# AdaLN plus mixture-of-LoRA feed-forward in split fp32: two of three column groups as a seven-product 2x2 block product per pair of tiles

## The reference

```
h   = gelu(gelu(cond @ W0 + b0) @ W1 + b1);  att = softmax(h @ W2 + b2)       # 32 x 8
y_b = (sum_k att[b,k] weight[k]) @ x_b + sum_k att[b,k] bias_k[k]             # 64x64 mix of channels per batch
p   = softmax(y @ gate_W.T); keep the top 2 of 8 experts, renormalised to w
out = x + y @ W_base.T + sum_e 2 w_e (y @ A_e.T) @ B_e                         # 1024 -> 1024, LoRA rank 8
```

## Time and profile before

| | |
|---|---|
| median of 3 runs | 257.17 us (257.11 to 258.16) |
| profiled execution, its own time | 257.24 us |
| its span, first to last instruction | 255.5 us |
| PE, PEld busy | 250.4 (98%), 243.0 (95%) us |
| DVE busy | 127.6 us (50%) |
| ACT busy | 87.7 us (34%) |
| POOL busy | 9.5 us (4%) |
| HBM | 137 GB/s over the span |
| mean granted TensorE clock | 1.000 |

### The profile page before, as it was taken

How to read it: one execution, slowest core, us unless ns; L and a number is a source line. 1 busy time by engine, 2 the same in 40 slices (tenths; PEclk the granted TensorE clock), 3 DMA queues, 4 the chain that set the end, 5 groups by cost and what they waited for, 6 DMA issues and landing times.

```text
span 255.5 us, 4274 instructions
## 1 busy us (share of the span) xinstructions
PE 250.4 (98%) x1456; PEld 243.0 (95%) x1456; DVE 127.6 (50%) x400; ACT 87.7 (34%) x205; POOL 9.5 (4%) x27
## 2 busy tenths in 40 slices
PE   8999999999999999999999999999999999999993
PEld 5899989898999999999999999999999999999992
DVE  2998643374845554345355444445545434535342
ACT  4677675816141231413132141324123141313120
POOL 6000042000000000000000000000000000000000
PEclk9999999999999999999999999999999999999999
DMA  6999868040551606051240706033060705122022
GB/s 176 406 403 316 346 176 305 17 164 3 225 185 48 201 1 246 1 176 70 86 160 0 246 0 227 19 117 129 38 208 0 244 3 174 75 87 77 3 82 82
DMA packets 10921, 35.27 MB, mean 138 GB/s; under 512 B 1264, under 2 KB 1824, under 8 KB 10912
## 3 DMA queue, kind: packets, MB, share of 16 engines
q1 hardware_dynamic: 10912, 35.15, 39.5%
HBM read 26.73 MB, written 8.39 MB: 137 GB/s over the span
## 4 chain that ended last, share of the span: by engine, by line
PE 98%; DVE 1%; issue 0%; POOL 0%; DVEq 0%; POOLq 0%
PE z_ps L764 25%; PE z_ps L765 25%; PE z_ps L766 25%; PE o_ps L783 3%; PE o_ps L789 3%; PE o_ps L788 3%; PE o_ps L780 3%; PE o_ps L778 3%; PE t_ps L843 2%; PE s_ps L813 1%; PE o_ps L764 1%; PE o_ps L765 1%; PE o_ps L766 1%; PE t_ps L804 0%; PE o_ps L892 0%; DVE z_lo L539 0%
## 5 line engine op out<-in xcount | busy, mean ns | idle before, releaser
L764 PE MATMUL z_ps<-w_hi,xt_hi 128*128 128x366 f32 (+1 forms) x376 | 125.8, 335 | 0.0
L765 PE MATMUL z_ps<-w_lo,xt_hi 128*128 128x366 f32 (+1 forms) x376 | 124.2, 330 | 0.0
L766 PE MATMUL z_ps<-w_hi,xt_lo 128*128 128x366 f32 (+1 forms) x376 | 124.0, 330 | 0.0
L764 PEld LDWEIGHTS z_ps<-w_hi,xt_hi 128*128 128x128 f32 x376 | 70.8, 188 | 0.7 <-issue 0.6
L765 PEld LDWEIGHTS z_ps<-w_lo,xt_hi 128*128 128x128 f32 x376 | 71.0, 189 | 0.2 <-issue 0.2
L766 PEld LDWEIGHTS z_ps<-w_hi,xt_lo 128*128 128x128 f32 x376 | 70.7, 188 | 0.0
L539 DVE TENSOR_TENSOR z_lo<-z_ps,z_hi 128x366 fp32r<-128x366 f32 (+1 forms) x47 | 25.3, 538 | 82.1 <-ACT z_hi L397 82.0
L397 ACT ACTIVATE z_hi<-z_ps 128x366 fp32r<-128x366 f32 (+1 forms) x47 | 22.4, 476 | 123.6 <-PE z_ps L766 123.6
L554 DVE TENSOR_TENSOR xt_lo<-xt_raw,xt_hi 128x1024 fp32r<-128x1024 f32 x14 | 17.2, 1225 | 17.7 <-ACT xt_hi L387 17.7
L617 DVE TENSOR_TENSOR out_sb<-o_ps,x_nat 128x366 f32<-128x366 f32 (+1 forms) x44 | 19.9, 505 | 4.5 <-PE o_ps L789 3.8
L778 PE MATMUL o_ps<-z_hi,blk_hi 128*128 128x366 f32 (+1 forms) x48 | 16.2, 338 | 0.0
(11 more groups left out here) (111 smaller groups left out, 178.8 us busy)
## 6 DMA issues: line engine op xcount, KB each, us to landing
x_nat<-x_in SPq DMA_DIRECT2D x16, 512.0 KB, 4.7
out<-out_sb SPq DMA_DIRECT2D x15, 512.0 KB, 3.0
xt_raw<-xt_in SPq DMA_DIRECT2D x14, 512.0 KB, 5.2
w_nat<-wn_in SPq DMA_DIRECT2D x8, 512.0 KB, 4.7
w_raw<-wext_in SPq DMA_DIRECT2D x8, 366.0 KB, 8.9
w_raw<-wext_in SPq DMA_DIRECT2D x4, 364.0 KB, 5.8
xt_raw<-xt_in SPq DMA_DIRECT2D x4, 256.0 KB, 5.4
par<-small_in SPq DMA_DIRECT2D x1, 576.0 KB, 7.2
```

The costliest lines, as they stand in the source:

```text
L764: nc.tensor.matmul(dst, hi, w_cols(w_hi, g, k), start=(k == 0), stop=False)
L765: nc.tensor.matmul(dst, hi, w_cols(w_lo, g, k), start=False, stop=False)
L766: last = nc.tensor.matmul(dst, lo, w_cols(w_hi, g, k), start=False, stop=(k == KC - 1))
```

## The change

Pairs 0 and 1 (tiles 0 to 3) stay as they were but for the following: lora_b always has 128 rows (bias rows zero until they are loaded, one small DMA for each of three rows and tile), and DVE and ACT make four sums of weight blocks there: `t_sum` (8 DVE subtractions of 128x732), `t_high` (8 ACT copies), `t_low` (8 DVE subtractions; the last four of them in the first part of pair 2).

From pair J0 = 2 on, both tiles of a pair are one unit. Let X be [[x0a, x0b], [x1a, x1b]] (tiles 0 and 1 of the pair, halves a and b of the contraction) and W the same for column groups 1 and 2. X @ W is made with seven block products of 12 matmuls (Winograd's form) in place of eight: four sums of x blocks (s_1 to s_4, 128x512; `ss_add` on DVE, `ss_high` on ACT, `ss_low` on DVE), four sums of weight blocks, and five `u_step` additions on DVE of 128x366 that join partial sums in PSUM with running sums u2, u3, c22 in SBUF. Group 0 (gate and A) stays a plain product (`z_zero`). `gating2` does the gating of both tiles with one set of instructions. Buffers of the new data lie over w_raw, w_nat and par, which are used up by then. SP reloads x tiles after the last sum that reads them.

Below, q = j - J0. `NP, NU, NO, NS = 7, 5, 6, 4` are the increments a pair of p_done, u_done, zz_hi/zz_lo/oo_done/ll_done/emptied, and s_*. Parts for the first and last pair are cut.

```diff
+            def ss_add(q, n):
+                a, b, op = {1: (xt_raw[:, 1, 0:D // 2], xt_raw[:, 1, D // 2:D], ALU.add), ...}[n]
+                nc.vector.tensor_tensor(s_raw[...][:, :], a, b, op).then_inc(s_added, 1)
+            def ss_low(q, n):                       # waits for ss_high n; s_lo = s_raw - s_hi
+            def xx_low(n, parity):                  # waits for xx_high; as x_low_next, 128x1024
+            def bb_low(q, t, parity):               # waits for bb_high; as block_low
+            def zz_low(n, src, g):
+                dve.wait_ge(zz_hi, n)
+                nc.vector.tensor_tensor(z_cols(z_lo, g), src, z_cols(z_hi, g).bitcast(F32), ALU.subtract).then_inc(zz_lo, 1)
+            def empty(n, bank, parity, g):          # waits for ll_done n; as one group of add_out
+            def u_step(out, a, b):
+                nc.vector.tensor_tensor(out[:, :], a[:, :], b[:, 0:WB], ALU.add).then_inc(u_done, 1)
+            def pair(j, ...):                       # DVE
+                    dve.wait_ge(p_done, NP * q)
+                    u_step(u2, u2, bank_c)
+                    xx_low(2 * q + 1, 1)
+                    zz_low(NO * q - 1, u2[:, :], 2)
...
+                    ss_add(q, 1)
+                    empty(NO * q - 3, o_ps[2], 0, 2)
+                    zz_low(NO * q, c22[:, :], 2)
+                    ss_add(q, 2)
+                    ss_low(q, 1)
+                    zz_low(NO * q + 1, bank_z[:, 0:WIDTH[0]], 0)
+                    empty(NO * q - 2, bank_f0, 1, 0)
+                    empty(NO * q - 1, o_ps[1], 1, 1)
+                    empty(NO * q, o_ps[2], 1, 2)
+                ss_low(q, 2)
+                ss_add(q, 3)
+                bb_low(q, 2 * j, 0)
+                bb_low(q, 2 * j + 1, 1)
+                ss_low(q, 3)
+                ss_add(q, 4)
+                zz_low(NO * q + 2, bank_c[:, 0:WIDTH[0]], 0)
+                ss_low(q, 4)
+                dve.wait_ge(p_done, NP * q + 2)
+                u_step(u2, u2, bank_b)
+                gating2(q, j, first)
+                u_step(u3, u2, bank_b)
+                u_step(c22, u3, bank_c)
+                xx_low(2 * q + 2, 0)
+                zz_low(NO * q + 3, bank_a[:, 0:WB], 1)
+                dve.wait_ge(p_done, NP * q + 6)
+                u_step(u3, u2, bank_b)
+                empty(NO * q + 1, o_ps[0], 0, 0)
+                empty(NO * q + 2, o_ps[1], 0, 1)
+                zz_low(NO * q + 4, u3[:, :], 1)
...
+            def pair(j, ...):                       # ACT
+                    act.wait_ge(u_done, NU * q)
+                    zz_high(q - 1, 5, u2[:, :], 2)
+                    act.wait_ge(p_done, NP * q)
+                    xx_high(j, 1)
+                ss_high(q, 1)
+                    act.wait_ge(oo_done, NO * q - 2)
+                    zz_high(q - 1, 6, c22[:, :], 2)
+                ss_high(q, 2)
+                act.wait_ge(zz_done, 2 * q + 1)
+                zz_high(q, 1, bank_z[:, 0:WIDTH[0]], 0)
+                ss_high(q, 3)
+                    act.wait_ge(oo_done, NO * q)
+                bb_high(2 * j, 0)
+                bb_high(2 * j + 1, 1)
+                zz_high(q, 2, bank_c[:, 0:WIDTH[0]], 0)
+                ss_high(q, 4)
+                nc.scalar.activation(u2[:, :], bank_a[:, 0:WB], ACT.Copy).then_inc(p1_copied, 1)
...
+                act.wait_ge(p_done, NP * q + 5)
+                    xx_high(j + 1, 0)
+                zz_high(q, 3, bank_a[:, 0:WB], 1)
+                tt_copy(q, 0); tt_copy(q, 1)
+                zz_high(q, 4, u3[:, :], 1)
...
+            def lora_pair(dst, i, cols):
+                nc.tensor.matmul(dst, lora_t[:, i, :], b_hi[:, cols], start=False, stop=False, skip_group_check=True)
+                return nc.tensor.matmul(dst, lora_b[:, i, :], b_lo[:, cols], start=False, stop=True, skip_group_check=True)
+            def product(bank, a, b, start=True, stop=True):   # 4 chunks x (hi*hi, hi*lo, lo*hi), then p_done
+            def mixed(bank, parity, g, n):                    # waits for zz_hi n and zz_lo n; as o_group
+            def pair(j, ...):                       # PE
+                z_zero(0, range(HK))                          # 12 matmuls; HK = 4 chunks
+                    mixed(o_ps[2], 0, 2, NO * q - 1)
+                    lora_out(o_ps[2], 0, 2)
+                    z_zero(0, range(HK, KC))
+                    mixed(o_ps[1], 1, 1, NO * q - 2)
+                    lora_out(bank_f0, 1, 0)
+                    lora_out(o_ps[1], 1, 1)
+                z_zero(1, range(HK))
+                    mixed(o_ps[2], 1, 2, NO * q)
+                    lora_out(o_ps[2], 1, 2)
+                z_zero(1, range(HK, KC))
+                pe.wait_ge(bb_lo, 4 * q + 2)
+                mixed(o_ps[0], 0, 0, NO * q + 1)
+                product(bank_a, x_part(0, 0), w_part(1, 0), stop=False)     # p1
+                product(bank_b, s_part(2), t_part(2))                       # p2
+                mixed(bank_f0, 1, 0, NO * q + 2)
+                product(bank_c, s_part(1), t_part(1), stop=False)           # p3
+                product(bank_b, s_part(3), w_part(2, 0), stop=False)        # p4
+                product(bank_a, x_part(0, 1), w_part(1, 1), start=False)    # p5
+                pe.wait_ge(gg_step, GG * (q + 1))           # then two transposes
...
+                product(bank_b, x_part(1, 1), t_part(4), start=False)       # p6
+                mixed(o_ps[1], 0, 1, NO * q + 3)
+                lora_out(o_ps[0], 0, 0)
+                lora_out(o_ps[1], 0, 1)
+                product(bank_c, s_part(4), w_part(2, 1), start=False)       # p7
```

More of the change, by code:

```diff
@@ L46 @@
 GS = 160
+WB = 366
+HK = 4
 TS = 256
@@ L437, in step, with t_high @@
-            def step(j, parity, last=False, sums=False):
+                nc.scalar.activation(lora_t[:, t % 2, :], t_ps[:, 0:P], ACT.Copy).then_inc(lora_t_ready, 1)
+                nc.scalar.activation(lora_b[0:ER, t % 2, :], t_ps[0:ER, 0:P], ACT.Copy).then_inc(lora_t_ready, 1)
+            def t_high(n, h):
+                dst, src = (t_hi[n][:, h * 2 * WB:(h + 1) * 2 * WB], T_RAW[n]) if n != 3 else (piece(w_hi, 8 + h), 8)
+                nc.scalar.activation(dst, piece(w_raw, src + h), ACT.Copy).then_inc(t_hi_ready, 1)
@@ L515, in _, with zz_high, ss_high @@
             step(1, 1)
[L516 to L522, removed]
+            def zz_high(q, n, src, g):
+                nc.scalar.activation(z_cols(z_hi, g), src, ACT.Copy).then_inc(zz_hi, 1)
+            def ss_high(q, n):
+                act.wait_ge(s_added, NS * q + n)
+                nc.scalar.activation(s_hi[n][:, :], s_raw[n % 2 if n != 4 else 1][:, :], ACT.Copy).then_inc(s_hi_ready, 1)
@@ new lines, in xx_high, with bb_high @@
+            def xx_high(j, parity):
+                act.wait_ge(xt_loaded[parity], j * 16)
+                nc.scalar.activation(xt_hi[:, parity, :], xt_raw[:, parity, :], ACT.Copy).then_inc(xx_hi, 1)
+            def bb_high(t, parity):
+                for s in range(2):
+                    rows = slice(CH * s, CH * (s + 1))
+                    nc.scalar.activation(blk_hi[rows, parity, rows],
+                                         agg[rows, bass.ds(t, 1), :].rearrange("p t c -> p (t c)"),
+                                         ACT.Copy).then_inc(bb_hi, 1)
@@ L525, in _ @@
+            pair(J0, first=True)
+            with act.Fori(J0 + 1, PAIRS - 1) as j:
+                pair(j)
+            pair(PAIRS - 1, last=True)
+            q = PAIRS - 1 - J0
+            act.wait_ge(u_done, NU * (q + 1))
+            zz_high(q, 5, u2[:, :], 2)
         @block.vector
@@ L733, in _ @@
             first_tile_out(2)
+            t_sum(1, 0)
+            t_sum(1, 1)
+            dve.wait_ge(t_add, 2)
             step(1, 0, early=True)
             step(1, 1, late=True)
[L736 to L744, removed]
@@ new lines, in _ @@
+            pair(J0, first=True)
+            with dve.Fori(J0 + 1, PAIRS - 1) as j:
+                pair(j)
+            pair(PAIRS - 1, last=True)
+            q = PAIRS - 1 - J0
+            dve.wait_ge(p_done, NP * (q + 1))
+            u_step(u2, u2, bank_c)
+            dve.wait_ge(xn_loaded[1], 16 * PAIRS)
+            dve.wait_ge(out_stored[1], 16 * (PAIRS - 1))
+            empty(NO * q + 3, bank_f0, 1, 0)
+            zz_low(NO * q + 5, u2[:, :], 2)
+            empty(NO * q + 4, o_ps[1], 1, 1)
@@ L751, in _ @@
+            empty(NO * q + 5, bank_a, 1, 2)
+            empty(NO * q + 6, o_ps[2], 0, 2)
         @block.tensor
@@ new lines, in _ @@
+            pair(J0, first=True)
+            with pe.Fori(J0 + 1, PAIRS - 1) as j:
+                pair(j)
+            pair(PAIRS - 1, last=True)
+            q = PAIRS - 1 - J0
+            pe.wait_ge(tt_copied, 4 * (q + 1))
+            pe.wait_ge(row_loaded[1], 48 * (PAIRS - 1))
+            lora_out(bank_f0, 1, 0)
+            pe.wait_ge(emptied, NO * q + 2)
+            mixed(o_ps[1], 1, 1, NO * q + 4)
+            lora_out(o_ps[1], 1, 1)
```

(5 more changed lines are left out.)

523 lines of the change are left out of this document (419 added, 104 removed).

## The result

The changed kernel takes 281.14 us (median of 4 runs, 278.32 to 285.64) against 257.67 of the kernel before beside it: ratio 1.0859 [1.0799, 1.0918], slower. The forecast was 268.3 in 260 to 276: the direction held, the size did not.

A forecast was written before the change was run, and what follows sets the result against it. PE's matmul stream was taken to bound the kernel. 257.24 - 12.1 - 2.3 + 10.2 + 8.0 + 3.0 + 4.5 = 268.5 us, taken as 268.3 for a little more overlap; range 260 to 276 with neighbours.

The forecast's parts named there:

- products: From pair 2 on, seven products of 12 matmuls replace eight in each of six pairs: 12.1 us saved.
- start: LoRA products of tiles 0 and 1 use 128 rows of lora_b instead of 64: 2.3 us saved.
- place one: PE waits before mixed(o_ps[2], 0, 2) for the remainder of u2: 2.04 us in each of five pairs, 10.2 us.
- place two: PE waits before mixed(o_ps[0], 0, 0) for the even tile's block remainders: 1.6 us in each of five pairs, 8.0 us.
- first pair: PE's wait before mixed(o_ps[0], 0, 0) in the first pair, behind a longer DVE queue: 3.0 us, bounds 2.5 and 4.1.
- place three: PE waits before mixed(o_ps[1], 0, 1) for the remainder of bank_a: 0.9 us in each of five pairs, 4.5 us.
- Clock: Rival: PE's clock falls in the stalls, 4 us a fall; one fall 272 us (chance 0.08), each pair 293 (0.04).
- DVE fills up: Rival: new instructions 20% longer or waits costlier, each stall 0.4 us longer, a fourth at gating: 275 us, chance 0.10.
- Covered: Rival: conversions keep ahead, PE stays dense, only the savings count: 242.8 us; chance 0.08 for covered or mostly covered.

The follow-up runs named there:

- experiment 2: Changed kernel with DVE making the remainder of u2 (zz_low) ahead of the x remainder (xx_low): 266.25 us, ratio 1.0237.
- experiment 3: Changed kernel with block steps first: bb_low ahead of the third empty on DVE, bb_high ahead of ss_high 3 on ACT: 262.23 us, ratio 1.0193.
- experiment 4: Changed kernel with the remainder of bank_a ahead of the x remainder, on ACT and DVE: 271.00 us, ratio 1.0518.
- experiment 7: Kernel of experiment 5 with ACT copying tile 1's z group 2 and LoRA coefficients ahead of the last row sums: 243.50 us, ratio 0.9437.
- Experiment 6: Kernel before the change with only the 128-row LoRA products of tiles 0 and 1 added: 256.49 us against 257.61, ratio 0.9944.
- experiment 1: Changed kernel with useless matmuls that PE runs while it would stand at the three stalls: 273.89 us, ratio 1.0619.
- experiment 5: Changed kernel with the reorderings of experiment 2, experiment 3 and experiment 4 together: 245.05 us, ratio 0.9505.

## Why the prediction was wrong, step by step

From the execution before to the one after, with measured terms: 257.24 - 12.1 (products) - 0.5 (start) + 10.4 (place one) + 9.5 (place two) + 3.2 (first pair) + 4.8 (place three) + 7.5 (slow stretches) = 280.0, and 280.91 was measured; 16 first matmuls behind a wait, each 0.25 in place of 0.168 us before its successor, account for 1.3 more, which makes 281.3 and leaves 0.4 us unexplained.

- *Fewer products, 12.1 us:* right. With the waits gone a pair takes 27.24 us (27.26 worked out).
- *Place one, 2.04 us x 5:* right, 2.07. The path took 4.08 us (4.06 worked out), and experiment 2 shows the cause named, the x remainder in front.
- *Place three, 0.9 x 5:* right, 0.97 (four times, 0.89 once).
- *First pair, 3.0:* right, 3.2.
- *Place two, 1.6 x 5:* mis-sized, 1.98 (1.57 once), 9.5 in place of 8.0. The wait was the right one (experiment 3); in the rows above the first step is 0.20 for 0.27 and the next four agree to 0.02 us, but from blk_hi to blk_lo it is 153.48 - 152.81 = 0.67 where 0.53 was set, and from the start of blk_lo to PE 0.83 where 0.50 was. Two blk_lo are half of the row's 1.02 us, so the handover to the idle PE took about 0.3 us, not the 0.06 of the earlier trace rows. At place one the same handover was 143.44 - 143.29 = 0.15. At place two PE's stream has three more waits between this one and the matmul; whether they make the difference no run tests.
- *Start, 2.3 saved:* wrong, 0.5 (transpose of tile 3 at 73.43, before at 73.94). Of the missing 1.8 us, 1.0 is the launch of this execution: its half-pace matmuls last to 11.7 us in place of 9.6, and tile 0's first LoRA matmul comes at 35.25 in place of 34.27. That is not the change's: with the same code up to there it came at 34.20 in experiment 4 and 35.49 in experiment 7. From that matmul to the transpose of tile 3, 1.5 us are saved (38.18 for 39.67). The step that failed is "PE has no idle time behind either place, so I take 2.3". Tile 1's saving is there. Tile 0's is there up to tile 1's transpose (7.83 us for 8.97) but spent before tile 1's LoRA matmuls (12.49 for 12.72). ACT's order shows the reason:

```profile
45.26 1.06 ACT L499 ACTIVATE w_nat<-w_nat 128x1024 f32<-128x1024 f32 x1 [1.26 <-DMA w_nat<-wn_in]
...
46.32 0.46 ACT L485 ACTIVATE z_hi<-z_ps 128x366 fp32r<-128x366 f32 x1
...
46.83 0.43 PE L1154 MATMUL o_ps<-z_hi,blk_hi 128*128 128x366 f32 x1 [0.47 <-ACT z_hi L485]
```

  PE came earlier and met a copy that stands behind a row sum, which waits for a DMA. The trace before had the bound: there the same copy ended at 45.63 + 0.46 = 46.09, only 0.28 us before PE used it.

```profile
45.63 0.46 ACT L397 ACTIVATE z_hi<-z_ps 128x366 fp32r<-128x366 f32 x1
...
46.37 0.33 PE L778 MATMUL o_ps<-z_hi,blk_hi 128*128 128x366 f32 x1
```

  Experiment 6 measures half of the term (1.1), experiment 7 takes the wait away.
- *Clock, left out of the sum:* this is the step that broke the range: with the stalls filled and no fall the time was 273.89 us (experiment 1), inside it. The rival named the mechanism and its place and was given 0.12 in all, "Against: the gaps are short, and PE streams between them". Experiment 1 shows that it holds with gaps of 2.2, 2.2 and 1.1 us a pair. Its price was wrong the other way: 4 us a fall were taken from the launch, where PE is slow for 8 us; a fall in the middle costs 1.5. Five falls are 7.5 us, and the forecast of 268.3 with these, place two's 1.5 and the start's 1.8 gives 279.1. That the clock falls with such gaps is shown; which gaps make it fall is not.
- *DVE fills up:* did not hold; its durations are those of their relatives (0.53, 0.69, 1.22 us), gating never made PE wait, and 177 us of DVE fit in 242.8.
- *Covered, 242.8 us:* false for this order of instructions, nearly true with the order mended; experiment 5 came to 244.49 in its profiled execution.

## What to carry to other kernels

When work is moved onto engines that run in order, follow each wait of the bottleneck back through the queue in front of its releaser: here three conversions stood behind operations whose results were needed only later, and three swaps turned 9% slower into 5% faster. Price stalls of PE with what follows them, since matmuls behind them may run at half pace: where several gaps come in each pass of a loop, put that case into the sum, not beside it. A saving on an engine that has no idle time lasts only up to the next operand that is just on time (here 0.28 us early); look for the operation that came last before it.

## What the runs showed of the hardware that was not expected

- Waits of PE of 0.8 to 1.9 us, three in a pair of 34 us, lowered the clock to 1.2 GHz for ten or eleven matmuls at a time, in four of five steady pairs. With the longest, the second or the shortest of the three gone it fell in none, one and one of five (experiments 2 to 4).
- The fall need not come at the longest gap's end: it began 0.6 us after the first matmul behind the 3.06 us wait (86.36 to 86.97), 0.9 us behind the one at 154.31, and 1.3 us behind the one at 181.13 of experiment 4.
- A weight load of 64 rows takes 0.18 us, one of 128 rows 0.19, and yet matmuls that alternate between the two come 0.36 us apart in place of 0.168, since their loads start together with them (experiment 6).
- The first matmul after a wait stands 0.25 us before its successor (143.44, 143.69), and so does the first one behind the matmuls that filled the stall (140.95, 141.20), so idle time alone does not explain it. In both its weight load starts only 0.03 us ahead of it, where in the stream a load starts 0.16 to 0.17 ahead (its successor's at 143.52 and 141.03). The loads, of the changed kernel and of experiment 1:

```profile
143.41 0.19 PEld L1347 LDWEIGHTS o_ps<-z_hi,blk_hi 128*128 128x128 f32 x1 [2.19 <-issue]
```

```profile
140.92 0.19 PEld L1347 LDWEIGHTS o_ps<-z_hi,blk_hi 128*128 128x128 f32 x1 [0.20 <-issue]
```
